# Edge terms and score tails from bfloat16 splits, and the multi head's running sums through PSUM

## The reference

```
h = relu(layernorm(x));  logit = tanh(h W1^T) w2
x = x + sum over edges into a node of softmax(logit[src]) * h[src]      # "pool"
h = relu(layernorm(x))
# two attention convolutions; key and value of an edge are k[src]+e and v[src]+e,
# with e = edge_attr @ We:
alpha = sum(q[dst] * (k[src] + e)) / sqrt(C)
agg   = segment_sum((v[src] + e) * softmax(alpha by dst))
out   = agg + (h Ws + bs)
# first convolution: 8 heads of 16 channels ("multi"), then relu;
# second: 1 head of 128 channels ("single");  result: x + out
```

## Time and profile before

| | us |
|---|---|
| median of 3 runs | 10849.4 |
| lowest and highest | 10781.99 and 10866.37 |
| span of the profiled execution | 7414.1 |
| the profiled execution's own time | not given by the page |
| PE, DVE, ACT, POOL busy | 5718.3, 4663.7, 3438.6, 4576.5 |
| DMA moved | 861.45 MB, mean 116 GB/s |

### The profile page before, as it was taken

The page is one execution under the profiler, slowest core; times in us unless marked ns, Lnnn a source line. Parts: engine busy times, 40 slices in busy tenths (PEclk is TensorE's granted clock), DMA queues, the critical chain, the costliest instruction groups (busy, mean ns, idle before and its releaser), DMA issues. The chain is left out here.

```text
span 7414.1 us, 172328 instructions
## 1 busy us (share of the span) xinstructions
PE 5718.3 (77%) x38285; PEld 4085.0 (55%) x38285; DVE 4663.7 (63%) x12926; ACT 3438.6 (46%) x8180; POOL 4576.5 (62%) x4707
## 2 busy tenths in 40 slices
PE   4555566666665688888888888856889999999998
PEld 3455555555542466666666666633555556666666
DVE  4444555555665788999999999933444555555542
ACT  3233333333443466666666666612444444444441
POOL 0777777777750477777666665502777777777630
PEclk7777878888986799999999999977999999999995
DMA  2334444444434666666655555534445555555532
GB/s 81 85 82 83 85 85 87 88 89 89 92 90 140 161 155 157 159 158 153 151 144 145 142 140 137 130 103 119 108 110 112 117 116 119 123 122 123 119 88 60
DMA packets 1267854, 861.45 MB, mean 116 GB/s; under 512 B 637234, under 2 KB 1158320, under 8 KB 1266840
## 3 DMA queue, kind: packets, MB, share of 16 engines
q1 hardware_dynamic: 1091672, 438.53, 25.3%
q0 software_dynamic: 175168, 411.90, 23.7%
HBM read 780.46 MB, written 69.42 MB: 115 GB/s over the span
## 5 line engine op out<-in xcount | busy, mean ns | idle before, releaser
L757 POOL DMA_INDIRECT ring_multi<-kv_rows,src_cols x1564 | 1609.3, 1029 | 1029.7 <-issue 440.4
L1155 POOL DMA_INDIRECT ring_single<-h_rows,src_cols x1564 | 1482.6, 948 | 857.2 <-issue 480.3
L1155 POOL DMA_INDIRECT ring_pool<-pool_rows,src_cols x1564 | 1482.0, 948 | 678.6 <-issue 451.5
L1258 PE MATMUL ps_s_pool<-ident,row_pool 128*128 128x128 f32 x1952 | 365.1, 319 | 718.0 <-ACT row_pool L1300 716.8
L1300 ACT ACTIVATE row_pool<-ring_pool 128x520 f32 x488 | 309.1, 633 | 1162.1 <-POOLq L1146 1162.1
L958 PE MATMUL ps_e_multi<-w_edge,attrT 64*128 64x512 f32 x976 | 544.5, 638 | 331.4 <-DVE kv L847 310.9
L1222 DVE CUSTOM_DVE_ANT_0 masked_pool<-mask_pool,ps_s_pool,start_pool 128x512 f32<-128x512 bf16 x488 | 364.8, 748 | 633.4 <-PE ps_s_pool L1258 552.3
L1271 PE MATMUL ps_p_pool<-row_pool,probT_pool 128*128 128x129 f32 x3904 | 667.1, 325 | 55.2 <-DVE probT_pool L1235 54.2
L847 DVE TENSOR_TENSOR kv<-ring_multi,ps_e_multi 128x1024 f32<-128x1024 f32 x488 | 596.1, 1222 | 161.6 <-issue 124.0
L1258 PEld LDWEIGHTS ps_s_pool<-ident,row_pool 128*128 128x128 f32 x1952 | 254.1, 160 | 801.5 <-issue 764.9
L1305 ACT ACTIVATE rowT<-ps_r 128x512 f32<-128x512 f32 x488 | 291.7, 598 | 816.4 <-PE ps_r L1265 816.4
(11 more groups left out here) (218 smaller groups left out, 12218.1 us busy)
## 6 DMA issues: line engine op xcount, KB each, us to landing
dst_pool<-in_dst_rows SPq DMA_DIRECT2D x488, 128.0 KB
dst_multi<-in_dst_rows SPq DMA_DIRECT2D x488, 128.0 KB
dst_single<-in_dst_rows SPq DMA_DIRECT2D x488, 128.0 KB
query_multi<-query_parts SPq DMA_DIRECT2D x488, 96.0 KB
cols<-query_cols SPq DMA_DIRECT2D x488, 64.0 KB
ring_pool<-pool_rows,src_cols POOLq DMA_INDIRECT x1564
ring_multi<-kv_rows,src_cols POOLq DMA_INDIRECT x1564
ring_single<-h_rows,src_cols POOLq DMA_INDIRECT x1564
```

Source lines behind the costliest of these rows:

```text
L757: pool.indirect_dma_start(out=ring[:, u, j, :], out_offset=None, in_=rows, in_offset=bass.IndirectOffsetOnAxis(ap=g.src_cols[:, c:c + 1], ...
L1155: pool.indirect_dma_start(out=ring[:, u, j, :], out_offset=None, in_=rows, in_offset=bass.IndirectOffsetOnAxis(ap=g.src_cols[:, c:c + 1], ...
L1258: i = T_.transpose(ps_s[p1][:, j * P:(j + 1) * P], row[:, u1, j, D + 1:D + 2].to_broadcast([P, P]), g.ident[:])
```

## The change

The 16 attributes of an edge, and in the single stage the 17 rows of `query_tail`, are written as the sum of three bfloat16 parts, which together carry the float32 value.

- The pool stage gets 40 extra chunks, one in 12 items: SyncE loads 626 columns of the attributes (with `We` of the first convolution behind them), ScalarE and VectorE make the three parts in turns, SyncE stores them to `edge_parts` in DRAM.
- Multi: attributes are loaded as bfloat16 parts, already with channels down the partitions, twice (2 x 48 rows of 512 edges). Transposition, `attrT` and the float32 matmul go; eight bfloat16 matmuls of 128 columns per item make `ps_e`. VectorE's L890 goes: L830 writes the scaled sums to `kept_sums`, TensorE adds them to `ps_p` with an identity matmul in float32, ScalarE copies `ps_p` back to `acc`.
- Fold: VectorE splits `query_tail` in five instructions after ScalarE's copy; SyncE stores it in 12 DMAs to `query_tails` in place of one.
- Single: the tail matmul becomes two in bfloat16, of 99 and 48 rows and 512 columns; the tail of queries is loaded in two DMAs, the edges' as 2 x 48 rows of parts.
- The input `edge_cols` of 17 rows gives way to `edge_flat`, 16 rows and the weight.

```diff
@@ -58,7 +58,17 @@
+SPLIT = 3
+SPLIT_K = SPLIT * EDGE_DIM
+CHANNEL = EDGES + P
+FLAT = EDGE_DIM * CHANNEL // P
+CHUNK_W = 626
+SPLITS = FLAT // CHUNK_W
+EVERY = 12
+TAIL_A = 2 * SPLIT_K + SPLIT
+TAIL_ROWS = TAIL_A + SPLIT_K
...
+assert SPLITS * CHUNK_W == FLAT and (SPLITS - 1) * EVERY + 18 < ITEMS
@@ -695,15 +708,16 @@
+            kept_sums = sb(g, ph, "kept_sums", [P, 2, H * HW])
...
-            attr = sb(g, ph, "attr_multi", [P, U, J, EDGE_DIM])
+            attr = sb(g, ph, "attr_multi", [2 * SPLIT_K, U, EDGES_B], BF16)
...
-            attrT = sb(g, ph, "attrT", [J * EDGE_DIM, 2, P])
-            w_edge = sb(g, ph, "w_edge", [J * EDGE_DIM, J, D])
+            w_edge = sb(g, ph, "w_edge", [2 * SPLIT_K, D], BF16)
+            w_last = sb(g, ph, "w_edge_last", [SPLIT_K, D], BF16)
@@ -768,10 +782,9 @@
-                sp.wait_ge(g.w_edge_clear, 1)
-                for j in range(J):
-                    sp.dma_start(w_edge[j * EDGE_DIM:(j + 1) * EDGE_DIM, j, :], t["L1_gnn_We0"])\
-                      .then_inc(g.w_edge_loaded, 16)
+                for a, dest in enumerate((w_edge[0:SPLIT_K], w_edge[SPLIT_K:2 * SPLIT_K], w_last[:])):
+                    sp.dma_start(dest, g.edge_parts[a * EDGE_DIM:(a + 1) * EDGE_DIM, EDGES:CHANNEL]
+                                 .unsqueeze(0).to_broadcast([SPLIT, EDGE_DIM, P])).then_inc(g.w_edge_loaded, 16)
@@ -786,9 +799,9 @@
-                    E["attrT" if multi else "partial"].wait(sp, n - U)
-                    sp.dma_start(attr[:, u], t["edge_attr_16"].rearrange("(k p) c -> p k c", p=P)[:, ds(b * J, J), :])\
-                      .then_inc(g.attrs_loaded[u], 16)
+                    E["edge"].wait(sp, n - U)
+                    sp.dma_start(attr[:, u], g.edge_parts[:, ds(b * EDGES_B, EDGES_B)]
+                                 .unsqueeze(0).to_broadcast([2, SPLIT_K, EDGES_B])).then_inc(g.attrs_loaded[u], 16)
@@ -827,7 +839,8 @@
                     a5h = a5.rearrange("p t (h c) -> p (t h) c", h=H)
-                    V.tensor_tensor(out=a5h, in0=a5h, in1=factor[:, f5].unsqueeze(2).to_broadcast([P, H, HW]),
+                    V.tensor_tensor(out=kept_sums[:, (u - 5) % 2].rearrange("p (h c) -> p h c", h=H), in0=a5h,
+                                    in1=factor[:, f5].unsqueeze(2).to_broadcast([P, H, HW]),
@@ -882,18 +895,6 @@
                      .then_inc(E["drop"].sem, 1)
-                if has(m5, ITEMS):
-                    a5 = a5.rearrange("p t c -> p (t c)")
-                    E["partial"].wait(dve, m5)
-                    if multi:
-                        E["scaled"].wait(dve, m5)
-                        i = V.tensor_tensor(out=a5, in0=a5, in1=ps_p[:, 0:acc_w], op=ALU.add)
-                    else:
-                        E["factor"].wait(dve, m5)
-                        E["summed"].wait(dve, m5 - 1)
-                        i = V.scalar_tensor_tensor(out=a5, in0=a5, scalar=factor[:, f5, 0:1],
-                                                   in1=ps_p[:, 0:acc_w], op0=ALU.mult, op1=ALU.add)
-                    i.then_inc(E["summed"].sem, 1)
@@ -945,18 +946,18 @@
                             rhs = row[:, u5, j, 0:acc_w]
-                        i = T_.matmul(ps_p[:, 0:acc_w], lhs, rhs, start=(j == 0), stop=(j == J - 1))
-                    i.then_inc(E["partial"].sem, 1)
-                if multi and has(n, ITEMS):
+                        T_.matmul(ps_p[:, 0:acc_w], lhs, rhs, start=(j == 0), stop=False)
+                    E["scaled"].wait(pe, m5)
+                    T_.matmul(ps_p[:, 0:acc_w], g.ident[:], kept_sums[:, p5], start=False, stop=True)\
+                      .then_inc(E["partial"].sem, 1)
+                if has(n, ITEMS):
                     loaded(pe, g.attrs_loaded, attrs_base, n, u, 32)
-                    E["onehot"].wait(pe, n - 1)
-                    T_.transpose(ps_s[0:J * EDGE_DIM, 0:P], attr[:, u].rearrange("p j c -> p (j c)"),
-                                 g.ident[:]).then_inc(E["attrT"].sem, 1)
-                if multi and has(n, ITEMS):
-                    E["attrT_sb"].wait(pe, n)
                     E["kv"].wait(pe, n - 1)
-                    T_.matmul(ps_e[:], attrT[:, u % 2], w_edge[:].rearrange("k j c -> k (j c)"),
-                              start=True, stop=True).then_inc(E["edge"].sem, 1)
+                    for j in range(J):
+                        e = attr[:, u, j * P:(j + 1) * P]
+                        T_.matmul(ps_e[:, j * D:(j + 1) * D], e, w_edge[:], start=True, stop=False)
+                        i = T_.matmul(ps_e[:, j * D:(j + 1) * D], e[0:SPLIT_K], w_last[:], start=False, stop=True)
+                    i.then_inc(E["edge"].sem, 1)
@@ -1033,16 +1035,16 @@
                                   scale=-1.0, bias=one[:]).then_inc(E["onehotT_sb"].sem, 1)
-                    E["attrT"].wait(act, n)
-                    E["edge"].wait(act, n - 2)
-                    S_.activation(attrT[:, u % 2], ps_s[0:J * EDGE_DIM, 0:P], ACT.Copy)\
-                      .then_inc(E["attrT_sb"].sem, 1)
...
                     S_.activation(onehot32[:, p3], onehot[:, u3], ACT.Copy).then_inc(E["onehot32"].sem, 1)
+                if has(m5, ITEMS):
+                    E["partial"].wait(act, m5)
+                    S_.activation(g.acc[:, ds(items.tile(m5), 1), 0:acc_w].rearrange("p t c -> p (t c)"),
+                                  ps_p[:, 0:acc_w], ACT.Copy).then_inc(E["summed"].sem, 1)
@@ -1168,12 +1180,28 @@
+        def chunk(n, at):
...
+            i, r = divmod(n - at, EVERY)
+            return i if not single and r == 0 and 0 <= i < SPLITS else None
...
+                i = chunk(n, 0)
+                if i is not None:
+                    if i >= 2:
+                        sp.wait_ge(third_done, i - 1)
+                    sp.dma_start(whole[:, i % 2], t["edge_flat"][:, i * CHUNK_W:(i + 1) * CHUNK_W])\
+                      .then_inc(split_loaded[i % 2], 16)
+                i = chunk(n, 18)
+                if i is not None:
+                    sp.wait_ge(third_done, i + 1)
+                    sp.dma_start(split_rows[:, :, i * CHUNK_W:(i + 1) * CHUNK_W], split[:, i % 2])\
+                      .then_inc(split_stored[i % 2], 16)
@@ -1182,22 +1210,28 @@
                       .then_inc(g.query_loaded[u % QB], 16)
-                    sp.dma_start(cols_tail[:, u % QB],
-                                 g.query_cols[ds(tile, 1), D:ACC_W, :].rearrange("t c n -> (t c) n"))\
+                    sp.dma_start(tail_a[:, u % QB], g.query_tails[ds(tile, 1), 0:TAIL_A, :].rearrange("t c n -> (t c) n"))\
+                      .then_inc(g.query_loaded[u % QB], 16)
+                    sp.dma_start(tail_b[:, u % QB],
+                                 g.query_tails[ds(tile, 1), TAIL_A:TAIL_ROWS, :].rearrange("t c n -> (t c) n"))\
...
                     E["partial"].wait(sp, n - U)
-                    sp.dma_start(edge_tail[:, u], t["edge_cols"][:, ds(b * EDGES_B, EDGES_B)])\
-                      .then_inc(g.attrs_loaded[u], 16)
+                    sp.dma_start(edge_tail[0:2 * SPLIT_K, u], g.edge_parts[:, ds(b * EDGES_B, EDGES_B)]
+                                 .unsqueeze(0).to_broadcast([2, SPLIT_K, EDGES_B])).then_inc(g.attrs_loaded[u], 16)
...
             rolled(sp, ITEMS, U, 0, step, items.begin)
+            if not single:
+                for k in range(2):
+                    sp.wait_ge(split_stored[k], 16 * len(range(k, SPLITS, 2)))
...
                 V.memset(row[:, :, :, ACC_W - 1:ACC_W], 1.0)
+                V.memset(edge_tail[2 * SPLIT_K:TAIL_A], 1.0)
@@ -1234,10 +1268,22 @@
+                i = chunk(n, 5)
+                if i is not None:
+                    dve.wait_ge(first_done, i + 1)
+                    V.tensor_tensor(out=whole[:, i % 2], in0=whole[:, i % 2], in1=split[:, i % 2, 0], op=ALU.subtract)\
+                     .then_inc(first_off, 1)
+                i = chunk(n, 9)
+                if i is not None:
+                    dve.wait_ge(second_done, i + 1)
+                    V.tensor_tensor(out=split[:, i % 2, 2], in0=whole[:, i % 2], in1=split[:, i % 2, 1],
+                                    op=ALU.subtract).then_inc(third_done, 1)
...
+            if single:
+                pe.wait_ge(g.acc_clear, 3)
@@ -1247,10 +1293,11 @@
                         E["rowT_sb"].wait(pe, m1)
-                        landed(pe, g.query_loaded, query_base, m1, u1, 32)
+                        landed(pe, g.query_loaded, query_base, m1, u1, 48)
...
                         landed(pe, g.attrs_loaded, attrs_base, m1, u1, 32)
-                        T_.matmul(ps_s[p1][:], cols_tail[:, u1 % QB], edge_tail[:, u1], start=False, stop=True)\
+                        T_.matmul(ps_s[p1][:], tail_a[:, u1 % QB], edge_tail[:, u1], start=False, stop=False)
+                        T_.matmul(ps_s[p1][:], tail_b[:, u1 % QB], edge_tail[0:SPLIT_K, u1], start=False, stop=True)\
@@ -1303,6 +1350,16 @@
+                i = chunk(n, 3)
+                if i is not None:
```

(35 more changed lines are left out.)

48 lines of the change are left out of this document (33 added, 15 removed).

## The result

The changed kernel took 10891.1 us (median of 20 runs, 10851.4 to 10942.5), the kernel before 10850.4 us beside it (20 runs, 10777.6 to 10905.6): a ratio of 1.0047, 95% interval 1.003 to 1.0064. A repeat on another chip gave 10872.2 against 10823.4 us, 1.005 [1.0033, 1.0067]; one of its 17 executions of the kernel before took 13521.3 us, at a granted clock of 1.0, and is left out of the ratio. The change costs 41 and 49 us; the forecast was 10788 us, a gain of 61.

A forecast was written before the change was run, and what follows sets the result against it. Gathers were taken to bind pool and early multi, VectorE late multi, gathers then TensorE single. Terms 2 - 68 + 53 - 48 = -61 us took 10849.4 to 10788 us; range 10650 to 10980.

The forecast's parts named there:

- The premise: Whole kernel: 3435 us of the median lie outside the 7414.1 us span or in other executions, and carry over unchanged.
- Pool stage, +2: Pool stage: 40 chunks of splitting fit under the gathers, costing 2 us for their edges; bound +25.
- the 120 that the text put as the most: Pool stage: cost if the gathers' cover for the 40 chunks failed, 40 x 3 us.
- Multi stage, -68: Multi stage: VectorE binds and loses an addition, while TensorE's shortening only covers; 68 us gained, bounds -110 to -20.
- the term of 68: Multi stage: VectorE's lost addition, 316 items x 0.21 = 66 us, plus 2 for the 164 early items.
- Fold, +53: Fold: splitting and 12 stores delay the next load 3.8 us; twelve cycles cost 46 us, the last stores 7.
- 43 to 76: Fold: bounds of its cost, +43 at 0.42 us per DMA issue and +76 at 0.57.
- Single stage, -48: Single stage: shorter TensorE weight loads leave gathers as floor, gaining 71 us less 23 given back; bounds -93 to +27.
- gave back 23 us: Single stage: deducted from the 71 us gain because SP's six DMAs, some 3.6 us, come close to 3.82 per item.
- D: Rival, whole kernel: the change adds more than it takes, without a DMA jam; +108 us, 10957; chance 0.10.
- A: Rival, attribute loads: a few DMA engines carry the broadcast and delay gathers; middle case +200 us, 11050; chance 0.15.
- B: Rival, timed runs: TensorE at 1.2 GHz binds, so its relief doubles; -980 to -1100 us, 9800; chance 0.08.

The follow-up runs named there:

- e16: The changed kernel with two of a block's four gathers left out in all three stages: 6831.9 us, 0.9218 of the kernel before.
- e2: The kernel before with only the multi head's edge terms taken from bfloat16 splits, and the pool stage's splitting chunks: 10746.9 us, ratio 0.993.
- e15: The kernel before with two of a block's four gathers left out in all three stages: 6539.6 us, ratio 0.8828.
- e4: The kernel before with eight more one-column bfloat16 matmuls in each multi-stage item, their results unread: 10917.8 us, ratio 1.0089.
- e5: The kernel before with one more float32 identity matmul of 128 columns in each multi-stage item, VectorE's addition kept: 10934.0 against 10837.9 us, ratio 1.0107.
- e7: The kernel with only the edge terms changed, plus a one-column TensorE-ScalarE-TensorE hand-over put back: 10940.5 us, 1.0091 of the kernel before.
- e6: The kernel before with the multi stage's running sums closed in PSUM, but copied back by VectorE instead of ScalarE: 10919.4 us, ratio 1.0074.
- e13: The kernel before with two of a block's four gathers left out in the pool stage: 9342.1 against 10582.4 us, ratio 0.8815.
- e14: The kernel before with the pool stage's 128 KB destination load replaced by a 1 KB load to one partition: 10564.7 us, ratio 0.9986.

## Why the prediction was wrong

*The premise* failed first: "So 3435 us lie outside the trace or belong to executions that went otherwise. My sum is made against the span, and I carry the 3435 us over unchanged". It was the second half of the first sentence, and then nothing can be carried over: a hidden cost there need not be hidden here. A median 46% above the span of its own trace says that the rows describe another execution.

*Pool stage, +2.* Held: within 26 us in five traces with the chunks (2874 to 2895 us against 2881 to 2900). With the gathers halved in the quick way, VectorE 85% busy (932.53 of 1100 us), the cover was gone and 59 us appeared, inside the 120 that the text put as the most.

*Multi stage, -68.* Wrong in sign: +15 to +39 us (3659 and 3638 against 3620 and 3624 on other chips whose before took about as long). The step that failed is TensorE's: "PE gets 0.27 us shorter and the transposition besides ...: worth nothing, it only covers". The eight matmuls were priced at 0.069 each, from twelve that are issued back to back in 0.83 us; they take 0.16. The two float32 passes with the identity come on top, and TensorE's item grows by 0.20 us at a granted clock of 1.00, where it was to shrink by 0.27 and the transposition, and by 0.47 with the lower clock that goes with it, for which the forecast had no term. And TensorE's time is not cover: a matmul with the identity alone costs 96 us, eight of one column 100. VectorE's addition, the term of 68, is worth 28 to 47. What kept the loss small was a step that the text gave no price: ScalarE's copy of attrT "and its wait" go, and that place is worth some 174 us, the wait for `onehot` with it.

The Trainium skill, "TensorE: Matmul & The Clock Gate", Back-to-back issue gap, has about 81 ns a matmul for a stream of weight loads and matmuls of 128 columns. The trace of e16 has 159 ns for these eight in the 363 items whose clock was 1.00, twice the page, and 56 ns for the twelve that fetch the queries: the spacing differs by pattern within one kernel.

*Fold, +53.* Right in its mechanism and inside 43 to 76: +57 in the first pair of traces, +68 beside e2 and beside e15. It is above +53 since only nine of a batch's twelve stores issue in the 0.47 that was taken for all, and the three of a single row in 0.75; the changed kernel's SP:

```profile
7192.65 1.39 SPq L1633 DMA_DIRECT2D query_tails<-query_tails_sb  x3
7194.08 0.74 SPq L1635 DMA_DIRECT2D query_tails<-query_tails_sb  x1
```

*Single stage, -48.* No gain: +12 to +38 us with the tails alone, and in the changed kernel 3154 and 3204 against 3127 to 3158 in seven kernels with the old tails. The step that failed is SP's: "with a sixth and a longer one some 3.6, too close to 3.82", for which the text gave back 23 us. The sixth DMA and the longer one make SP's queue the bound of the whole stage in both ways of running: 4.15 us an item in the quick way, and some 6.5 in the long one (SP waits 26 us from 7600 to 10200 us in the changed kernel, and 736 in the kernel before, traced again). TensorE's relief itself came, 0.7 us an item of recorded time, and was idle time at once.

*The sum.* Measured, the terms are pool -26 to +14, multi +15 to +39, fold +57 to +68, single -4 to +77, against +2, -68, +53, -48. They add up to more than the +41 and +49 measured; they come from single traces on several chips, the upper ones from an execution 37 us above its median.

*The rivals.* D, "the change adds more than it takes", is what came, at half its size. A did not: with the broadcast alone multi got faster. B had the place right for the multi stage (TensorE, at a low granted clock), but its consequence, twice the relief, did not follow: TensorE's recorded busy time is 66% of the span before and 62% after, and cutting it by the tails gave nothing, since SP's queue came next.

Shown by runs: that the multi stage follows TensorE's work (e4, e5) and the place where TensorE stops for ScalarE and `onehot` (e7), that the sums' loop over ScalarE is not the cost (e6), that the fold costs its +68, that standstills in the pool stage go with the gathers (e13) and not with other traffic (e14). Read from traces, without a run that takes it away: that SP's queue bounds the single stage. Open: why an unchanged kernel on one chip runs at 7407 us one time and at 10545 another, by what path gathers and TensorE's late signals hang together, and what the change does at 7407 us with all gathers.

## What to carry to other kernels

Before summing costs on a trace, hold its span against the median; if they differ by more than the runs do, price nothing by the trace's slack. Price a matmul by the distance between starts in the same pattern of weight load and matmul, not by a packed group's mean, and count an engine as cover only where its queue has been seen to stand idle on work that is not due. A round trip from TensorE over another engine and back can be worth more than any of the operations in it; take it off the chain first. Before adding a DMA to a stage, look how long its queue still waits for room in each item.

## What the runs showed of the hardware

- Leaving out half of the gathers of a stage, 766 of 1564, with all other work the same, shortened it by 1199 us in the long way (2808 to 1609), 1.6 us a gather, and by 731 us in the quick one (1971 to 1239), 0.95 us a gather; the gather engine itself is busy 0.95 us with one. Taking away other DMA traffic moved nothing.
- One chip ran the same kernel in 10545 us (one execution) and later in 7407 us (seven).
- In the quick way none of 7436 signals of TensorE comes more than 0.25 us after its matmul's recorded end; in the long way 2468 of 6662 come more than 1 us after. SP's register instructions take at most 0.07 us in the one, and up to 1.4 us in the other.
- Eight matmuls of 128 columns with 96 or 48 rows start 159 ns apart at a granted clock of 1.00 and 217 ns apart at 0.50.
- A DMA that repeats 48 rows for two copies (96 KB) occupies SP's queue 0.66 us, the plain one of 17 rows (34 KB) 0.25; a store of one row spread over seven tiles 0.75, of sixteen rows 0.43.
